# Causal masks of two self attentions as extra contraction rows and 32x32 products, and a cross attention that starts one step earlier

## What is computed

```
scores = einsum('bhqd,bhkd->bhqk', q, k) / sqrt(16)
scores = where(tril, scores, -inf)      # query q sees keys k <= q
out    = einsum('bhqk,bhkd->bhqd', softmax(scores), v)
```

## Time and profile before

| | us |
|---|---|
| median of 3 executions | 576.19 (575.97 to 577.64) |
| the profiled execution, device time | 570.98 |
| its span in the trace | 569.2 |

### The profile page before, as it was taken

The page is one execution under the profiler, slowest core; times in us unless marked ns, Lnnn a source line. Parts: engine busy times, 40 slices in busy tenths (PEclk is TensorE's granted clock), DMA queues, the critical chain, the costliest instruction groups (busy, mean ns, idle before and its releaser), DMA issues.

```text
span 569.2 us, 13098 instructions
## 1 busy us (share of the span) xinstructions
PE 535.0 (94%) x4933; PEld 341.4 (60%) x4933; DVE 360.8 (63%) x795; ACT 259.6 (46%) x533; POOL 319.5 (56%) x395
## 2 busy tenths in 40 slices
PE   7999998999999999999998999987999998899998
PEld 4556765444656666665665566664555554466687
DVE  5456864999865555543487567776687757972341
ACT  2315553000395666563454355645566567104530
POOL 3448754989675444331044699859799973540000
PEclk9999999999999999999999999999999999999999
DMA  8996028000006333331303994011120022028311
GB/s 279 109 133 282 3 102 372 0 0 1 0 7 223 111 95 108 96 108 55 99 27 47 124 196 167 1 30 29 43 91 2 2 70 99 1 86 303 122 45 59
DMA packets 25134, 53.05 MB, mean 93 GB/s; under 512 B 3515, under 2 KB 16333, under 8 KB 23153
## 3 DMA queue, kind: packets, MB, share of 16 engines
q1 hardware_dynamic: 24357, 51.01, 32.7%
q10 hardware_dynamic: 716, 1.21, 0.6%
HBM read 41.51 MB, written 1.12 MB: 75 GB/s over the span
## 4 chain that ended last, share of the span: by engine, by line
PE 62%; DVE 17%; POOL 8%; ACT 5%; issue 4%; SPq 2%; DMA 1%; ACTq 0%; POOLq 0%; DVEq 0%
PE PS L1394 57%; POOL R L614 6%; PE PS L1398 4%; DVE R L1240 4%; DVE R L1237 3%; DVE mx L1141 2%; DVE R L424 2%; DVE xn L1029 1%; SPq L445 1%; PE PS L1417 1%; ACT xnT L754 1%; POOL rstd L563 1%; PE PS L1853 1%; DVE X L1019 1%; DVE stats L1014 1%
## 5 line engine op out<-in xcount | busy, mean ns | idle before, releaser
L1394 PE MATMUL PS<-R 128*128 128x256 f16 (+5 forms) x1864 | 184.6, 273 | 2.7 <-DVE R L1296 1.4
L1394 PEld LDWEIGHTS PS<-R 128*128 128x128 f16 (+4 forms) x1864 | 123.1, 102 | 70.6 <-issue 42.2
L1141 DVE TENSOR_REDUCE mx<-PS 128x4 bf16<-128x512 f32 x128 | 82.4, 686 | 36.5 <-PE PS L1394 27.3
L840 ACT ACTIVATE R<-PS 128x512 f32<-128x512 f32 x128 | 69.4, 594 | 65.3 <-PE PS L1394 65.1
L1394 PE MATMUL PS<-xnT,R 128*128 128x512 f16 (+1 forms) x348 | 83.3, 379 | 1.4 <-ACT xnT L754 1.4
L614 POOL TENSOR_TENSOR R<-mx,causal 128x512 bf16<-128x512 bf16 x64 | 65.5, 1044 | 31.7 <-DVE mx L1141 30.3
L1287 DVE TENSOR_TENSOR R<-R,wr 128x512 f32<-128x512 f32 (+1 forms) x46 | 33.3, 723 | 57.3 <-ACT R L939 53.6
L614 POOL TENSOR_TENSOR R<-mx,R 128x512 bf16<-128x512 bf16 x64 | 65.3, 1043 | 6.3 <-DVE mx L1141 6.2
L939 ACT ACTIVATE R<-PS,small 128x512 f32<-128x512 f32 (+1 forms) x50 | 34.3, 686 | 48.9 <-PE PS L1394 48.9
L1394 PEld LDWEIGHTS PS<-xnT,R 128*128 128x128 f16 (+1 forms) x348 | 33.8, 99 | 33.6 <-ACT xnT L754 2.0
L1394 PE MATMUL PS<-negidb,R 128*128 128x128 bf16 x512 | 41.9, 219 | 3.8 <-ACT R L840 2.0
(11 more groups left out here) (206 smaller groups left out, 819.2 us busy)
## 6 DMA issues: line engine op xcount, KB each, us to landing
R<-in_experts_dram SPq DMA_DIRECT2D x5, 1536.0 KB, 8.3
R<-R SPq DMA_DIRECT2D x48, 128.0 KB, 7.0
wr<-g_scr SPq DMA_DIRECT2D x16, 256.0 KB, 3.2
R<-in_w_dram SPq DMA_DIRECT2D x1, 3200.0 KB, 17.5
R<-in_w_dram SPq DMA_DIRECT2D x1, 3168.0 KB, 10.3
WT<-in_wt_a_dram SPq DMA_DIRECT2D x2, 1024.0 KB, 11.7
R<-in_toe_dram SPq DMA_DIRECT2D x1, 2048.0 KB, 13.9
wr<-g_scr SPq DMA_DIRECT2D x10, 192.0 KB, 2.8
```

Source lines behind the costliest of these rows:

```text
L840: s.activation(PTm[:, n % 4, 4 * k:4 * k + 4, :], bank(2 + (2 * n + k) % 3).rearrange("p (h q) -> p h q", h=4), ACT.Exp, scale=c["sc"]).th ...
L1141: v.tensor_reduce(mx[:, n % 4, 4 * k:4 * k + 4], bank(k).rearrange("p (h k) -> p h k", h=4), AX.X, ALU.max).then_inc(S("att_mx"), 1)
L1394: return nc.tensor.matmul(o_, l, r, start=start, stop=stop)
```

## The change

- The tokens of a batch are taken as four blocks of 32 (`QUARTER`). Four extra contraction rows (48 to 51 and 112 to 115) are put in `QS` and `KS`: for each row, +65504 at the queries up to the end of its block and -65504 at the keys past it, so that their product masks whole later blocks. A product then has 52 rows for 48. POOL makes these rows (`blocks`, 4 partitions, 1024 columns for each of two) with four operations right after the identity. For the first attention SP copies them, repeated over the 8 head groups, with four DMAs in place of the former wait for the first weights; it also parks them in DRAM, and for the second attention loads four pieces from there once the first experts are done. The load of ctxT moves behind the first stacking.
- Inside the 32x32 blocks on the diagonal the mask is added by products of 32 rows by 32 columns, over 4 heads x 32 = 128 columns: `later_keys` after `scores`, eight of them, and `later_keys_by_key` after `scores_by_key`, eight more with the transposed mask `causal_k`. Each group k has its own row tile and bank.
- For the self attentions the 512-column mask products and POOL's `LMs` go. `less_max` takes the maximum itself, one column repeated 128 times, as stationary operand. `scores_by_key` goes before `scores` in a step. DVE's ring of maxima waits for `att_st`. The cross attention keeps its masks.
- The four fillers in each run's first `less_max` go; steps 1 to 6 of each run get fillers at their end: 6 in step 1, 2 in each other.
- `CROSS_FROM` goes from 20 to 19. For q = 0 the twelve spreading DMAs are divided: SP issues three for each cc as soon as this cc is there, and ACT the other three, after its exponentials in the step behind the one of the projection.

```diff
-CROSS_FROM = 20
+CROSS_FROM = 19
...
+        blocks = R2[0:4, 12288:12288 + T].bitcast(F16).rearrange("p (w n t) -> p w n t", w=2, n=B)
...
-            return [(8 * (u % 2) + 2 * j + k, 64 * k, 48, 4 * (u % 2) + j) for k in range(2) for j in range(4)]
+            return [(8 * (u % 2) + 2 * j + k, 64 * k, 52, 4 * (u % 2) + j) for k in range(2) for j in range(4)]
...
             load(WTs[0][:, :, :, :], A["wt_a0"], "w_a0")
-            sp.wait_ge(S("w_a0"), 16)
-            load(ctxT[:, :, :], A["ctxT"], "ctxT_loaded")
+            sp.wait_ge(S("blocks"), 1)
+            for which, to in ((0, QS), (1, KSa)):
+                for row in (48, 112):
+                    sp.dma_start(to[row:row + 4, :, :],
+                                 blocks[:, which].rearrange("p n t -> p (n t)").unsqueeze(1).broadcast_to(
+                                     [4, 8, T])).then_inc(S("blocked"), 16)
...
             stack(SELF0)
+            load(ctxT[:, :, :], A["ctxT"], "ctxT_loaded")
...
+            for which in range(2):
+                sp.dma_start(blocks_scr[which]...).then_inc(S("blocks_parked"), 16)
...
+            sp.wait_ge(S("down0"), N0)
+            sp.wait_ge(S("blocks_parked"), 32)
+            for which, to in ((0, QS), (1, KSb)):
+                for row in (48, 112):
+                    sp.dma_start(to[row:row + 4, :, :].rearrange("p g t -> p (g t)"),
+                                 blocks_scr[which]).then_inc(S("blocked"), 16)
             stack(SELF1)
...
+                if q == 0:
+                    for cc in range(DC):
+                        sp.wait_ge(S("qx_hi"), cc + 1)
+                        sp.wait_ge(S("qx_lo"), cc + 1)
+                        sp.wait_ge(S("att_st"), past(SELF1, "st") + 2 * SELF1["upb"])
+                        for term, part in enumerate((0, 0, 1)):
+                            spread(QS[:, :, ts], 64 * cc + 8 * term, qx[0:64, part, cc, ts], 8, "qx_stacked0")
+                    continue
...
+            link(g.memset(blocks[:, 0], HUGE))
+            link(g.affine_select(out=blocks[:, 0], in_=blocks[:, 0], compare_op=ALU.is_ge, fill=0.0,
+                                 base=QUARTER - 1, pattern=[[0, B], [-1, P]], channel_multiplier=QUARTER))
+            link(g.memset(blocks[:, 1], -HUGE))
+            g.affine_select(out=blocks[:, 1], in_=blocks[:, 1], compare_op=ALU.is_ge, fill=0.0, base=-QUARTER,
+                            pattern=[[0, B], [1, P]], channel_multiplier=-QUARTER).then_inc(S("blocks"), 1)
...
-                    if c:
-                        if c is CROSS:
-                            pool.wait_ge(S("xmask"), 1)
-                        else:
-                            pool.wait_ge(S("const"), 4)
+                    if c is CROSS:
+                        pool.wait_ge(S("xmask"), 1)
...
+            def first_queries(cc):
+                act.wait_ge(S("qx_hi"), cc + 1)
+                act.wait_ge(S("qx_lo"), cc + 1)
+                act.wait_ge(S("att_st"), past(SELF1, "st") + 2 * SELF1["upb"])
+                for term, part in enumerate((0, 0, 1)):
+                    row = 64 * cc + 32 + 8 * term
+                    act.dma_start(QS[row:row + 8, :, 0:256], qx[64:P, part, cc, 0:256]).then_inc(S("qx_stacked0"), 16)
...
+            dve.wait_ge(S("blocks_parked"), 32)
...
+                def on_diagonal(i, row, corner):
+                    rows = slice(row, row + QUARTER)
+                    for first in range(0, P, QUARTER):
+                        cols = slice(first, first + QUARTER)
+                        ins = mm(PS[cols, i, :].rearrange("p (j w) -> p j w", j=4)[:, :, cols], identb[rows, rows],
+                                 corner[rows, rows].unsqueeze(1).broadcast_to([QUARTER, 4, QUARTER]), False, True)
+                    return ins
+                def later_keys(c, u):
+                    for k in range(2):
+                        ins = on_diagonal(k, QUARTER * k, causal)
+                    ins.then_inc(S("att_s"), 1)
+                def later_keys_by_key(c, u):
+                    n = number(c, u)
+                    for k in range(2):
+                        ins = on_diagonal(2 + (2 * n + k) % 3, QUARTER * (2 + k), causal_k)
+                    ins.then_inc(S("att_st"), 1)
...
-                        if (c, u) == (run[0][0], 0) and k == 1:
-                            keep_busy(4, 2 + (i + 1) % 3)
-                        pe.wait_ge(S("att_lm"), i + 1)
+                        if c is CROSS:
+                            pe.wait_ge(S("att_lm"), 2 * u + k + 1)
+                        else:
+                            pe.wait_ge(S("att_mx"), i + 1)
...
-                            mm(PS[:, 2 + i % 3, j * P:(j + 1) * P],
-                               LMs[:, n % 3, 4 * k + j, :], negidb[:, :], j == 0, False)
+                            most = (LMs[:, n % 3, 4 * k + j, :] if c is CROSS
+                                    else mx[:, n % 4, 4 * k + j:4 * k + j + 1].broadcast_to([P, P]))
+                            mm(PS[:, 2 + i % 3, j * P:(j + 1) * P], most, negidb[:, :], j == 0, False)
...
+                    if older and older is not CROSS:
+                        scores_by_key(older, of)
                     if c:
-                        mask(c, u)
+                        operands_ready(c, u)
+                        if c is CROSS:
+                            mask(c, u)
                         scores(c, u)
-                    if older:
+                    if c and c is not CROSS:
+                        later_keys(c, u)
+                    if older is CROSS:
                         scores_by_key(older, of)
+                    elif older:
+                        later_keys_by_key(older, of)
...
                     if t == 0:
                         keep_busy(6, 4)
+                    elif t < 7:
+                        keep_busy(6 if t == 1 else 2, 6)
```

More of the change, by code:

```diff
@@ L639, in _ @@
             g.tensor_scalar(negidb[:, :], ident[:, :], -1.0, None, ALU.mult).then_inc(S("const"), 1)
+            link(g.memset(causal_k[:, :], 0.0))
+            link(g.affine_select(out=causal_k[:, :], in_=causal_k[:, :], compare_op=ALU.is_ge, fill=NEG, base=0,
+                                 pattern=[[1, P]], channel_multiplier=-1))
             link(g.memset(causal[:, :], 0.0))
@@ L842, in attention @@
                                          ACT.Exp, scale=c["sc"]).then_inc(S("att_exp"), 1)
+                    if run is SECOND:
+                        for q, cc in QUERIES.get(t - 1, []):
+                            if q == 0:
+                                first_queries(cc)
                     if run is SECOND and t == LAST_UNIT + 4:
@@ L1487, in attention, with operands_ready @@
             def attention(run):
-                def mask(c, u):
-                    upb = c["upb"]
-                    b, first = divmod(u, upb)
+                def operands_ready(c, u):
+                    b, first = divmod(u, c["upb"])
                     if c is CROSS and first == 0 and b % 2 == 0:
@@ L1513, in scores @@
                         for k in range(2):
+                            if c is not CROSS and j == 0 and n >= 1:
+                                pe.wait_ge(S("att_mx"), 2 * n + k - 1)
                             _, row, rows, idx = unit_heads(c, u)[4 * k + j]
                             ins = mm(PS[:, k, j * P:(j + 1) * P], QS[row:row + rows, idx, ts],
-                                     c["KS"][row:row + rows, key_at(c, idx), ts], False, j == 3)
-                    ins.then_inc(S("att_s"), 1)
+                                     c["KS"][row:row + rows, key_at(c, idx), ts], c is not CROSS and j == 0,
+                                     c is CROSS and j == 3)
+                    if c is CROSS:
+                        ins.then_inc(S("att_s"), 1)
                 def less_max(c, u):
```

40 lines of the change are left out of this document (24 added, 16 removed).

## The result

The changed kernel took 581.06 us in the median of 11 runs (575.66 to 583.15), the kernel before 576.19 beside it: a ratio of 1.0073, 95% interval 1.0041 to 1.0105. It is slower; 570.6 (565.0 to 576.5) had been forecast. Its profiled execution took 577.76 us, span 575.7. Both kernels spread by several us from execution to execution, so of a single profile only its stages are compared.

The account below looks back on a forecast made before the run. PE was taken to bound the first self attention, POOL the cross attention. 2 x (-1.3) + 2 x (-1.0) - 1.0 + 1.0 - 1.0 = -5.6 gave 565.4 profiled, 570.6 us as median; range 565 to 576.5.

Parts of the forecast that it names:

- Part 4: Start: POOL's four new operations delay rstd and first normalisation; SP's four issues fall in idle time; +1.0, between 0 and 2.
- the price of nothing for the load of ctxT and the copies behind the stacking: After the first stacking: ctxT, 1 MB, due only in the convolution, and the copies to DRAM cost nothing.
- Part 1: PE work of a self unit: masks removed, small products and a tiling change added; -0.19 a unit, -1.3 a run.
- -0.35 of the first unit: First unit of a self attention loses both masks for one tiling change and its corner products: -0.35.
- +0.4 of steps 16 and 17: Steps 16 and 17 have no mask to lose but still the older units' corner products: +0.4.
- Rivals A and B: Slower: A, repeated columns load slowly, 579.4 or 590, chance 0.10; B, small products go in turn, 590, chance 0.05.
- Part 2: First steps of each self attention: maximum to next scores 0.88 becomes 0.75, steps 2.17 become 2.04; -1.0 a run.
- Part 3: Second self attention: POOL does two 1.04 us operations a unit less, so PE's wait for low parts goes; -1.0.
- fills at half price: Lower bound for POOL's four start operations: 16-bit fills at half price, select as at 320 columns; 2.1, hidden.
- Part 5: Cross attention one step earlier, its first mask no longer waiting for a transfer: -1.0, between -2.9 and +1.1.
- POOL's extra work: Cross attention: one batch's rstd and row addition more on POOL, 1.5 together, half counted: +0.8.
- The base: Profiled execution of 570.98 would become 565.4; the 0.9% by which the median exceeds it was carried over, giving 570.6.

Follow-up runs that it names:

- the fastest kernel: Changed kernel with mask pieces split, first queries on SP, shared weights earlier, four large loads after the first self attention's last scores, expert loads later: 567.19 us, ratio 0.9869.
- the second: The kernel before, unchanged, profiled a second time: 575.88 us, first self maximum at 40.66 us.
- the repaired kernels: Changed kernel with first queries on SP, shared weights earlier and mask pieces moved; cross attention 82.97 (567.19 us with large loads later) or 83.06 (573.22 us without).
- pieces: Changed kernel, but SP waits for the first weights before issuing the four mask pieces: 577.34 us, ratio 1.0039.
- pieces split, queries, weights: Changed kernel with QS pieces after the first weights, KSa pieces between stacking halves, first queries on SP, shared weights before the last queries: 573.22 us, ratio 0.9969.

## Why the prediction was wrong

Its sign was wrong, though the terms on which it spent most words held. Two steps failed: Part 4's cost of the four mask-piece issues ("nothing due"), and the price of nothing for the load of ctxT and the copies behind the stacking. In their place the runs showed a first projection 2 to 4 us late with a start at half clock, and stops of PE for instructions under the loads.

- **Part 1** (-0.19 a unit): right. -0.23; the small products cost 0.20 with their change for 0.25 forecast. Without gaps the first self attention takes 37.38 for 39.66 from first to last maximum, -2.28. Parts 1 and 2 give about the same for this stretch, -2.35, as their -0.35 of the first unit and +0.4 of steps 16 and 17 lie outside it. Rivals A and B fell: loads 98 ns, products side by side. In the step shown above the small products begin at 66.07, before the 52-row ones end by their row (66.14): so nothing in it shows the drain at a change of mode that the Trainium skill ("TensorEngine Tiling (Array Packing)", Tiling Modes) states. As the ends of products are modelled in such rows, no run here decides it. The range of column steps that the Trainium skill gives for fast loads of bf16 operands ("TensorE: Matmul & The Clock Gate", Weight-path perf modes) holds the step of 0, and the 98 ns agree with it.
- **Part 2** (2.17 to 2.04): 2.06. Right.
- **Part 3** (-1.0): right once PE does not stop. The second attention of the fastest kernel takes 39.09 with a gap that makes one step 0.93 longer; less that, it is 3.2 under before for 3.3 forecast.
- **Part 4** (+1.0, up to 2) failed in its cause and its size. "SP's four issues, 4 x 0.65, fall between the weights' issue and the first stacking, where it has nothing due": they took 1.67 each, and I looked at SP's queue only. The pieces met the weights, which came 2 to 4 us later, and the two loads of ACT, whose issue held ACT's first copy. The prediction did name the weights, with an upper end of +2 in all. PE's idling then halved the clock for 10 us, 2.8 more. The cost was +7.45 against the first profile and +2.65 against the second. The term that was priced, POOL's, came to nothing: its four operations took 4.05 us for 4.6, and DVE normalised at 7.76 for 8.5. No run shows fills at half price, the lower bound there; they took 0.94 for the 1.15 in proportion to columns.
- **Part 5** (-1.0): wrong in its sum, -0.92 and +0.99, nothing. The earlier step itself is worth 1.6. "ACT's three issues ... +1.1": PE's wait was 2.15. And I did not ask who else counts in the moved step: the user of the shared weights does, 1.6 to 2.8 us of PE. POOL's extra work cost at most the +0.57 by which the cross attention grew in the repaired kernels.
- **What was put at nothing:** the supply of instructions. I wrote that ctxT's load "moves behind the stacking and is due only in the convolution" and that the copies "ride there too", at a price of nothing, asking only who waits for the data. 28 more PE instructions a unit and a DMA share near 1 in the same 20 us gave gaps of 0.7 to 3 us, some followed by half clock. This was the largest loss: 5 us of the time.
- **The base:** I carried the 0.9% between profile and median over as a constant. It is a matter of how long the clock stands at half in a run, and the change moved it: median clock 0.988, where the 29 runs of the kernel before have 0.997.

Repair by repair the ratios fall: 1.0073, 1.0039 (pieces), 0.9969 (pieces split, queries, weights), 0.9869 (loads). The intervals of the first three overlap from each to the next; that of the last stands apart. With the repairs the forecast of 570.6 is beaten, by 3.4 us.

What is shown: that the gaps go with the loads, end at instruction packets, and are absent from the kernel before. That the requests for instructions queue behind the loads' packets is argued from the packets' times. Not shown: how much of it is ctxT's load, which the change put there, and how much the three loads that the kernel before had there too; no run moved ctxT's alone. Open too: why some runs lose clock in the experts, and which part of the start's variation lies in the first loads of X.

## What to carry to other kernels

When an edit replaces few wide instructions by many small ones, count the instruction stream as traffic: look whether a large load runs in the same stretch, and move it to one where PE issues few (the convolution has 51 products in 20 us). When a stage is moved by a step, list every consumer whose step is reckoned from it and every producer whose step is not. Before taking a profile as the base, profile it twice: a start that waits on its first loads can differ by 5 us.

## What the runs showed of the hardware

A 16 KB instruction packet that lands late stops PE in the middle of a row of like products, shown as "issue", and PE resumes 1.2 to 1.55 us after it. One such packet comes for about 256 products and loads of PE. A DMA issue can hold the issuing engine's own work: ACT's issue of the rows table took 0.94 to 3.51 us in four profiles in which SP issued transfers to four partitions beside it, and 0.44 to 1.00 in those without. A stationary operand that is one bf16 column repeated 128 times loads in 98 ns, as the plain one before did, and sixteen 32x32 products take 0.20 us with a change of tiling. The granted clock fell to half at 10.7 us, while PE idled from 8.98 to 13.63; it also fell around idling of under 3 us, and in seven profiles in the experts, where PE had no gap. The same kernel started at full and at half clock in two executions.
